# Attention: score maxima of two key chunks joined in one instruction and moved by a DMA into one row, the next sequence's norm and transposes in small pieces

## What is computed

```python
x = x + mix(norm(x))          # a softmax mixing over tokens, from means of x
x = x + experts(norm(x))      # 8 experts, each picks 256 tokens a sequence
x = x + attention(norm(x))    # 16 heads of 64, causal, then @ w_o
x = x + experts(norm(x))
# attention, per head: a = q k^T / 8, masked above the diagonal
#                      y = softmax(a) v ; out = concat(y) @ w_o
```

## Time and profile before

| | |
|---|---|
| median of 3 runs | 2518.96 us (2515.04 to 2521.3) |
| the profiled execution's own time | 2510.51 us |
| its span in the profile | 2508.7 us |
| mean granted clock of TensorE | 0.947 |
| attention (first transpose of maxima to the last) | 761.0 to 1952.4 us |

### The profile page before, as it was taken

One profiled execution on the slowest core, in us unless ns is written; L12 is line 12 of the kernel. 1 busy time (PEld: TensorE's weight loads), 2 busy tenths in 40 slices (PEclk: granted clock), 3 DMA queues, 4 the chain that ended last, 5 costly groups with the idle time before them and its releaser, 6 DMA issues.

```text
span 2508.7 us, 33816 instructions
## 1 busy us (share of the span) xinstructions
PE 2272.5 (91%) x12104; PEld 1689.4 (67%) x12104; DVE 1564.3 (62%) x3334; ACT 1005.1 (40%) x1900; POOL 1293.3 (52%) x1043
## 2 busy tenths in 40 slices
PE   2888599989979999999999999999999768999997
PEld 1344488879976666676666766567566557888997
DVE  6325368865546777557775577764777444885563
ACT  2311154344434445435454344534455314434443
POOL 1000355566624766546664476644667433656664
PEclk9798689999998999999999999999999798999999
DMA  5131244455532221122111222123221214445552
GB/s 193 38 130 42 85 118 122 115 130 136 122 92 61 53 57 51 51 76 60 51 51 51 76 53 57 51 68 100 72 73 34 76 36 142 120 100 135 145 125 51
DMA packets 148454, 213.25 MB, mean 85 GB/s; under 512 B 19248, under 2 KB 112448, under 8 KB 148288
## 3 DMA queue, kind: packets, MB, share of 16 engines
q1 hardware_dynamic: 123712, 177.51, 23.8%
q0 software_dynamic: 24576, 33.57, 7.8%
HBM read 137.51 MB, written 39.98 MB: 71 GB/s over the span
## 4 chain that ended last, share of the span: by engine, by line
PE 74%; DVE 11%; POOL 5%; issue 5%; DMA 2%; ACT 2%; POOLq 1%; SPq 0%; DVEq 0%; ACTq 0%
PE psum L960 11%; PE psum L939 11%; PE psum L1064 9%; PE psum L988 7%; PE psum L1017 6%; PE psum L1036 5%; PE psum L1047 5%; PE psum L824 4%; PE psum L1085 4%; PE psum L1002 4%; PE psum L1074 2%; POOL t_acc L1762 2%; PE psum L857 1%; DVE f_hhi L1535 1%; PE psum L907 1%
## 5 line engine op out<-in xcount | busy, mean ns | idle before, releaser
L1239 ACT ACTIVATE t_p<-psum 128x512 f32<-128x512 f32 (+3 forms) x768 | 324.8, 491 | 359.9 <-PE psum L1047 354.8
L1762 POOL TENSOR_TENSOR t_acc<-t_acc,t_p 128x1024 f32<-128x1024 f32 (+3 forms) x256 | 415.7, 1624 | 19.2 <-ACT t_p L1239 0.8
L1582 DVE CUSTOM_DVE_ANT_0 psum<-psum,t_mask 128x128 f32<-128x128 f32 (+3 forms) x512 | 240.2, 510 | 150.9 <-PE psum L1017 150.9
L960 PE MATMUL psum<-f_whi,f_hhi 128*128 128x256 f32 x1024 | 299.8, 293 | 20.0 <-DVE f_hlo L1537 19.9
L1535 DVE CAST f_hhi<-f_h 128x512 fp32r<-128x512 f32 x256 | 161.6, 631 | 228.4 <-ACT f_h L1190 227.0
L960 PE MATMUL psum<-f_whi,f_hlo 128*128 128x256 f32 x1024 | 294.0, 287 | 0.0
L960 PE MATMUL psum<-f_wlo,f_hhi 128*128 128x256 f32 x1024 | 293.9, 287 | 0.0
L1064 PE MATMUL psum<-t_p,t_v 128*64 128x512 f32 (+3 forms) x1536 | 291.2, 500 | 1.5 <-POOL t_p L1742 1.5
L1687 POOL TENSOR_TENSOR f_wlo<-f_wst,f_whi 128x1024 fp32r<-128x1024 f32 x64 | 159.4, 2505 | 251.8 <-ACT f_whi L1174 251.7
L1190 ACT ACTIVATE f_h<-psum 128x512 f32<-128x512 f32 x256 | 153.1, 598 | 284.3 <-PE psum L939 249.3
L1762 POOL TENSOR_TENSOR t_acc<-t_p 128x768 f32<-128x768 f32 x64 | 134.9, 2108 | 174.5 <-PE psum L1074 170.1
(11 more groups left out here) (199 smaller groups left out, 4577.2 us busy)
## 6 DMA issues: line engine op xcount, KB each, us to landing
f_wst<-in_L_ffn_w SPq DMA_DIRECT2D x64, 1024.0 KB, 5.5
t_ka<-t_ka SPq DMA_DIRECT2D x64, 256.0 KB, 3.5
t_qb<-t_qa SPq DMA_DIRECT2D x64, 256.0 KB, 3.6
t_wk<-wkT SPq DMA_DIRECT2D x32, 256.0 KB, 4.2
t_wq<-wqT SPq DMA_DIRECT2D x32, 256.0 KB, 4.1
t_wv<-wvT SPq DMA_DIRECT2D x16, 512.0 KB, 4.8
normal<-f_xy SPq DMA_DIRECT2D x5, 1024.0 KB, 6.8
a_x<-in_L_attn_a_x SPq DMA_DIRECT2D x4, 1024.0 KB, 9.7
```

The costliest lines, as they stand in the source:

```text
L960: m = pe.matmul(out, h[:, js], w[:, f, :], start=(f == 0 and a == 0 and j % 2 == 0), stop=(f == FT - 1 and a == 2), skip_group_check=True)
L1239: act.activation(p[:, i, q0:], k.bank[bank][:, q0:], ACT.Exp, scale=1.0 / float(np.sqrt(k.DH))).then_inc(k.drained[bank], 1)
L1582: s = dve.tensor_tensor_reduce(part, part, t["mask"][:, BANK - w:BANK], 1.0, NEG, ALU.add, ALU.max, top)
L1762: pool.tensor_tensor(acc[:, :, q0:], (p0 if kt == 1 else acc)[:, :, q0:], p[:, :, q0:], ALU.add).then_inc(k.p_acc, 1)
```

## The change

The tiles `pick` and the semaphore `d_max` go; `mx` becomes one plain 128 x 128 tile with the 16 maxima in its first columns, `neg` ([16, 128], two of them) is new, the `qb` of two heads lie side by side in one tile, and `QROWS` is 65. `xres` is no tile of its own any more: its two chunks are the two halves of `xy`. The part of the key chunk with the diagonal takes the maximum of the full chunk, `mx1`, as its start value. `norm` has four steps of two bn_stats instead of two of four, everywhere it is used.

```diff
@@ -226,8 +232,9 @@
         t["rden"] = [sb("t_rden", [P, BANK // 32]) for _ in range(2)]
-        t["mask"], t["pick"] = sb("t_mask", [P, BANK], BF16), sb("t_pick", [NBLK, NBLK, P], BF16)
-        t["mx"] = [sb("t_mx", [P, 2, P // 2]) for _ in range(2)]
+        t["mask"] = sb("t_mask", [P, BANK], BF16)
+        t["neg"] = [sb("t_neg", [2 * NBLK, P], F32R) for _ in range(2)]
+        t["mx"] = [sb("t_mx", [P, P]) for _ in range(2)]
@@ -269,14 +276,24 @@
-        for n in range(self.NBLK):
-            for c in range(n // self.KPC + 1):
-                w = min(BANK, (n + 1) * P - c * BANK)
...
+        first = [(n, 0) for n in range(self.KPC + 1)]
+        rest = [(n + c, 1 - c) for n in range(self.KPC, self.NBLK) for c in (1, 0) if n + c < self.NBLK]
+        for n, c in first + rest:
...
@@ -569,13 +586,15 @@
             self.t_load(b)
+            for _ in range(4):
+                yield
...
         def normalize_results():
+            while state["stored"] < NC * (B - 1):
+                yield
             for b in range(B - 1):
-                while state["stored"] < NC * (b + 1):
-                    yield
@@ -613,9 +632,8 @@
                 state["values"] = project_values(b)
-            if hp == NHP - 2 and b + 1 < B:
+            if hp == NHP - 5 and b + 1 < B:
                 normalizing[b + 1] = normalize(b + 1)
-                extra.append(normalizing[b + 1])
@@ -675,11 +695,14 @@
                 if n == per * u:
+                    finish(n)
                     yield
-                    finish(n)
+                self.high_scores(u, c, kt)
+                if n == per * u:
...
                 yield
+                self.high_scores(u, c, kt + 1)
@@ -709,19 +732,21 @@
                 if place < 8:
-                    for _ in range(1 + (hp == 0 and place < 4)):
-                        pump(products)
+                    pump(products)
...
                     next(state["values"])
-                if 7 < place < 20:
-                    owed += 21 / 12
+                if 5 < place < 20:
+                    owed += 21 / 14
...
                         owed -= 1
+                if u + 1 < U and (place == 22 or (u + 2) % NHP == 0 and place > 19):
+                    pump(coming)
                 if place == 22 and u + 1 < U:
-                    pump(coming)
                     self.max_rows(u + 1)
-                if behind and place % 4 == 0:
+                if u // NHP + 1 in normalizing and place in (0, 2, 4, 6):
+                    pump(normalizing[u // NHP + 1])
+                if behind and place in (0, 2, 4, 6, 10, 14, 20, 21, 23):
@@ -1006,8 +1031,9 @@
         k, pe, t = self.k, self.e, self.k.t
+        if c == 0 and n % k.KPC == 0:
+            self.wait_drained(("qk", u, k.NC + n // k.KPC))
         if (n, c) == (0, 0):
-            self.wait_drained(("qk", u, 2 * k.NC - 1))
@@ -1021,27 +1047,37 @@
         bank = self.take(("rows", u), self.work_bank())
-        self.wait_ge(k.t_const_p, 6)
-        self.wait_ge(k.d_max, u + 1)
-        pe.transpose(k.bank[bank][:, 0:P], t["mx"][u % 2][:].rearrange("p i n -> p (i n)"),
-                     k.ident[:]).then_inc(k.filled[bank], 1)
+        self.wait_ge(k.t_const_p, 4)
+        for n, c, _, heads in k.max_parts():
+            if c == n // k.KPC:
+                self.wait_drained(("max", u, n, c, heads[0]))
+        pe.transpose(k.bank[bank][:, 0:P], t["mx"][u % 2][:], k.ident[:]).then_inc(k.filled[bank], 1)
...
+    def high_scores(self, u, c, kt):
+        k, pe, t = self.k, self.e, self.k.t
+        q0, qs, ks = self.score_slices(c, kt)
+        for i in range(2):
+            bank = self.take(("st", u, c, kt, i), self.work_bank())
+            hd = t["heads"][u % 2][i]
+            pe.matmul(k.bank[bank][:, q0:], hd["ka"][:, ks], hd["qa"][:, qs], start=True, stop=False)
...
         k, pe, t = self.k, self.e, self.k.t
-        banks = [self.take(("st", u, c, kt, i), self.work_bank()) for i in range(2)]
...
-        for i in range(2):
-            hd = t["heads"][u % 2][i]
-            pe.matmul(k.bank[banks[i]][:, q0:], hd["ka"][:, ks], hd["qa"][:, qs], start=True, stop=False)
+        q0, qs, ks = self.score_slices(c, kt)
+        banks = [k.where["st", u, c, kt, i][0] for i in range(2)]
...
             v = min(4 + 2 * hp, 16) - 1
-            self.wait_drained(("rows", u))
...
                 self.wait_ge(k.q_dup[u % 2][h][1], DMA * (u // 2 + 1))
+            self.wait_ge(k.q_rows[u % 2], DMA * (u // 2 + 1))
@@ -1568,36 +1604,31 @@
         k, dve, t = self.k, self.e, self.k.t
-        mx, mx1 = t["mx"][u % 2], t["mx1"]
+        mx, mx1 = k.maxima(u), t["mx1"]
...
             self.wait_filled(("rows", u - 2))
-        if (n, c) == (k.KPC, 1) and u:
-            self.wait_ge(k.d_max, u)
...
         for i in heads:
-            top = mx1[:, i, n - k.KPC:n - k.KPC + 1] if c else mx[:, i, n:n + 1]
...
             if c == n // k.KPC:
-                self.wait_ge(k.t_const_p, 6)
-                s = dve.tensor_tensor_reduce(part, part, t["mask"][:, BANK - w:BANK], 1.0, NEG, ALU.add, ALU.max, top)
+                self.wait_ge(k.t_const_p, 4)
+                if c:
+                    self.wait_drained(("max", u, n, 0, i))
+                s = dve.tensor_tensor_reduce(part, part, t["mask"][:, BANK - w:BANK], 1.0,
+                                             mx1[:, i, n - k.KPC:n - k.KPC + 1] if c else NEG, ALU.add, ALU.max,
+                                             mx[:, i, n:n + 1])
             else:
-                s = dve.tensor_reduce(top, part, AX.X, ALU.max)
+                if u:
+                    self.wait_drained(("max", u - 1, n, 1, k.heads_of(n, 1, i)))
+                s = dve.tensor_reduce(mx1[:, i, n - k.KPC:n - k.KPC + 1], part, AX.X, ALU.max)
         s.then_inc(k.drained[bank], 1)
-        if (n, c, i) == (k.NBLK - 1, 1, 1):
-            for m, d, _, h in k.max_parts():
-                if m >= k.KPC:
-                    self.wait_drained(("max", u, m, d, h[0]))
-            dve.tensor_tensor(mx[:, :, k.KPC:k.NBLK], mx[:, :, k.KPC:k.NBLK], mx1[:], ALU.max).then_inc(k.d_max, 1)
...
         bank = self.wait_filled(("rows", u))
-        for i in range(2):
-            self.wait_ge(k.t_const_p, 6)
...
-            s = dve.tensor_tensor(t["heads"][u % 2][i]["qb"][k.DH:k.QROWS, :].rearrange("p (a b) -> p a b", b=P),
-                                  spread(rows, 1, k.NBLK), t["pick"][:], ALU.mult)
-        s.then_inc(k.drained[bank], 1)
+        if u > 1:
+            self.wait_ge(k.q_rows[u % 2], DMA * (u // 2))
+        dve.tensor_scalar(t["neg"][u % 2][:], k.bank[bank][0:2 * k.NBLK, 0:P], -1.0, None, ALU.mult).then_inc(k.drained[bank], 1)
@@ -1907,7 +1935,8 @@
         else:
-            self.wait_filled(("xT", k.B - 1, 1, 1))
+            for c in range(k.NC):
+                self.wait_ge(k.q_xout[c], DMA * (k.B - 1))
@@ -1924,6 +1953,9 @@
         self.wait_filled(("xT", b - 1, 1, 1))
+        if b > 1:
+            for c in range(k.NC):
+                self.wait_ge(k.q_xout[c], DMA * (b - 1))
@@ -1954,11 +1986,22 @@
+    def max_rows(self, u):
+        k, sp, t = self.k, self.e, self.k.t
+        if u > 1:
+            self.wait_filled(("st", u - 2, 1, 2 * k.KPC - 1, 1))
+        self.wait_drained(("rows", u))
+        row = t["qb"][u % 2][k.DH:k.QROWS, :, :].rearrange("p i (n j) -> p (i n) j", j=P)
+        sp.dma_start(row.bitcast(F32), t["neg"][u % 2][:].bitcast(F32)).then_inc(k.q_rows[u % 2], DMA)
...
         k, sp = self.k, self.e
-        if b:
-            self.wait_ge(k.q_xout[c], DMA * b)
-        sp.dma_start(k.t["xres"][c][:], self.chunk(k.res, b, c)).then_inc(k.q_xres[c], DMA)
+        if b + 1 < k.B:
+            self.wait_filled(("xT", b + 1, 1, 1))
+        else:
+            self.wait_ge(k.q_y[b - 1], DMA * 2)
+        sp.dma_start(k.t["xres"][c], self.chunk(k.res, b, c)).then_inc(k.q_xres[c], DMA)
```

More of the change, by code:

```diff
@@ L208, in attention_tiles, with heads @@
         L, D, NBLK, DT, DH, NHP, KPC = self.L, self.D, self.NBLK, self.DT, self.DH, self.NHP, self.KPC
[L209 removed]
+        t["qb"] = []
+        def heads():
+            qb = sb("t_qb", [P, 2, L], F32R)
+            t["qb"].append(qb)
+            return [dict({n: sb("t_" + n, [P, L], F32R) for n in ("qa", "ka", "kb")}, qb=qb[:, i, :]) for i in range(2)]
         values = lambda: sb("t_v", [P, NBLK, 4 * DH])
@@ L218, in attention_tiles @@
         t["v"].append(values())
-        t["xres"] = [sb("t_xres", [P, KPC, D]) for _ in range(2)]
+        t["xres"] = [t["xy"][:, c * KPC:(c + 1) * KPC, :] for c in range(2)]
         t["stats"], t["mv"], t["rstd"] = (sb("t_stats", [P, NBLK, 6]), sb("t_mv", [P, NBLK, 2]),
@@ L338, in norm @@
         self.runs += 1
-        for half in range(2):
-            self.norm_stats(n, half, x, stats, mv, rstd, ready)
+        for part in range(4):
+            self.norm_stats(n, part, x, stats, mv, rstd, ready)
             yield
@@ L1275, in norm_stats @@
```

(6 more changed lines are left out.)

35 lines of the change are left out of this document (18 added, 17 removed).

## The result

After: 2474.59 us, median of 4 runs (2469.95 to 2480.52). Before beside it: 2517.0 us (2510.6 to 2521.3). The ratio is 0.9835, interval 0.9804 to 0.9866: 1.65% faster, 42 us. In a later comparison of 6 runs against 11 it was 0.9851 (0.9819 to 0.9883). The prediction was 2494 us with a range of 2478 to 2510. The sign was right; the gain was bigger than the range allowed, by 3.4 us. Executions of one kernel scatter by 10 us and more here, and the two profiled ones are 35.0 us apart.

The account below looks back on a forecast made before the run. TensorE, busy 91% of the span, was taken as the bound, others costing only where it waits. Terms 20 + 4.5 + 3 + 2 - 4.5 + 0 = 25 us off 2510.5 gave 2485.5; plus 8.5 to the median, 2494 us, range 2478 to 2510.

Parts of the forecast that it names:

- D: Lighter VectorE in ordinary units: weight loads wait less for the low halves; gain 2 us over 25 units.
- A: Next sequence's norm, in smaller steps and started earlier, stops stalling TensorE in three units; gain 20 us, bounds 11 and 22.
- B: Next sequence's transposes, moved earlier behind other matmuls, no longer make TensorE wait; gain 4.5 us, bounds 0 and 6.5.
- C: Attention's output product, two places later, avoids waits for t_yT and the one put down to issue; gain 3 us.
- E: Last sequence's norms of results: 1 MB loads and a store delay the key doubling; loss 4.5 us, bounds +8 and -10.
- F: New row DMA in every unit, ready at T+2.0 to T+2.9 (T: maxima transpose's start), before the low score matmul; cost 0.
- My own test of that premise: Sign for the whole kernel: VectorE's busy time down 100 us with unchanged span would disprove that TensorE's waits were VectorE's doing.
- the unit interval that I named as proof: Sign for F: ordinary units staying at 34.0 to 34.1 us, the low score matmul at T+2.96 without a DMA wait.
- the row DMA was not late: Rival on the low score matmul's path: landing at 3.5 us gives 2530 us; chance 0.07 slower, 0.04 near break-even.
- the norm didn't stall: Rival on the next sequence's norm: it still stalls in the low halves' window, half of A lost, 2505 us; chance 0.13.
- E didn't gain: Rival on the last sequence's norms: the doubling doesn't stand behind the loads, gain 6 us, total 2483; chance 0.13.
- the loads of t_xy and xres behind it held up none of TensorE's lines: Rival that gains only move: t_xy load delays the doubling, xres makes waits, E goes badly; 2514 us, chance 0.05.

Follow-up runs that it names:

- join alone: The kernel before with only the joined maxima, their new order, the scaling by -1 and the row DMA, old schedule kept: 2513.32 us.
- ballast run: The changed kernel with two idle VectorE products per unit behind the scaling of the maxima: 2519.07 us, before beside it 2524.82.
- the pieces alone: The kernel before with only the new schedule of norm and transposes: 2477.64 us once, later 2486.59 us (6 runs), ratio 0.9883.

## Why the prediction was too careful

The median came out 19.4 us below the forecast of 2494. Of these, 10.0 are the terms: I forecast 25 us, and the profiled executions are 35.0 apart. The other 9.4 are the step from one profiled execution to a median: I added 8.5 us to the sum because before's profiled execution lay that far below its median, and after's lies 1.0 above its own. That 8.5 was scatter taken for an offset. With the terms right and that offset kept, the forecast would have been 2484, so the measured time would still have lain 9 us below it; the medians of 11 and 6 runs later differ by 36.8.

In attention the gain was 40.6, with a loss of 7.0 behind it. The terms, with the ordinary unit's 0.54 us taken out of each row of the table and counted under D:

| part | forecast | measured |
|---|---|---|
| A, norm in small pieces | 20 | 25.9 - 9 x 0.54 = 21.0 |
| B, transposes | 4.5 | 13.3 - 6 x 0.54 = 10.1 |
| C, output two places later | 3 | 2.8 - 4 x 0.54 = 0.6 |
| D, lighter VectorE | 2 | 26 x 0.54 + 3.1 = 17.1 |
| E, norms of results | -4.5 | -4.6 - 7 x 0.54 = -8.4 |
| F, row DMA | 0 | 0 |
| tail | not looked at | -7.0 |

- **The step that failed is D**, sized at 2 us where the profile has 17.1: "the matmul slips about 0.1 us. Over 25 units: gain 2". I took an ordinary unit for TensorE's alone because it was "busy without a break". The ends of matmuls are modelled, so a chain of matmuls that start a little late shows as busy. The one visible sign was the weight load's 0.27 us, which I cut to 0.1; matched matmul by matmul, TensorE lags by 0.28 from there on, and the unit gave 0.54 in all (0.13 of it by the wider spacing of the row maxima, which the forecast didn't price). My own test of that premise was the other way round (VectorE falls, the span doesn't), and the unit interval that I named as proof, 34.0 to 34.1, came out at 33.50. The join alone and the ballast run put the cause in the VectorE work ahead of the low halves, with the ballast's size only roughly matched.
- **A was right in size** by the sum, and in mechanism: in after the waits of L1013 and L1067 for t_kb are 2.2 us where L988 and L1036 had 16.1. Units 5, 13 and 21 take 33.50 us each, where one took 41.47; units 4, 12 and 20 take 0.5 to 0.7 more than ordinary ones, about the 0.5 a sequence that I left for GpSimd's pow. I missed that the new start is also a condition for F: without it the row DMA makes the norm units 12.0 us longer (the join alone), through the load behind it on SyncE. And the pieces alone bring 15, not 20; the rest needs the lighter VectorE that A's text counted as room.
- **B was mis-sized**: 10.1 against 4.5, above its bound of 6.5. The place is worth 4.0 when VectorE is light and 6.6 when it isn't; the rest is D again, in units in which VectorE has more to do.
- **C** brought 0.6, since its last wait was 2.2 us and not nothing, and it made the tail longer.
- **E was right in mechanism, and low.** In unit 25 I had the doubling issued near T+7.5 and landed at T+18.8, and a stall from T+14.6, 4.2 us long; in unit 28 a stall of 5.7 to 7.6. Timelines of SyncE and TensorE in after; T is 1687.31 and 1802.41:

```profile
1694.50 0.38 SPq L1940 DMA_DIRECT2D t_xy<-out  x1
1694.99 1.17 SPq L1987 DMA_DIRECT2D t_ka<-t_ka  x2
1706.26 0.66 PE L1043 MATMUL psum<-t_ka,t_qa 128*128 128x128 f32 x2 [4.27 <-DMA t_ka<-t_ka]
...
1803.97 0.53 SPq L1945 DMA_DIRECT2D normal<-t_xy  x1
1808.43 0.38 SPq L1940 DMA_DIRECT2D t_xy<-out  x1
1808.91 1.18 SPq L1987 DMA_DIRECT2D t_ka<-t_ka  x2
1818.56 0.66 PE L1043 MATMUL psum<-t_ka,t_qa 128*128 128x128 f32 x2 [4.66 <-DMA t_ka<-t_ka]
```

  The first is right to 0.2 us (doubling issued at T+7.68, TensorE on at T+18.95, 4.27). The second is 1.0 short of the low end, since the store landed in 4.5 us and TensorE went on 9.7 us behind the doubling's issue. The loss was 8.4 and not 4.5, near the far bound of 10. Beside the 8.9 us of stalls there is a lower clock: 0.92 in units 25 and 28 and 0.95 in unit 29, where the other four have 1.00. Units 26 and 27 are 1.9 and 1.4 us longer than with the loads held back, at full clock, and that isn't explained. The windows (columns as in the earlier trace rows) of the unit shown above and of 44 us from the first load on:

```profile
1160.28:1193.76 33.48, 33.30 (x178) 22.42 (x177) 24.45 (x63) 16.78 (x36) 22.94 (x22) 1.00 0.20 48
1694.00:1738.00 44.00, 39.13 (x190) 26.82 (x188) 27.34 (x75) 17.80 (x39) 24.67 (x22) 0.92 0.26 61
```

- **F was right.** Scaling 0.28 us against 0.25, issue at T+0.62 against T+0.6, landing 1.8 us, inside the 1.4 to 2.3 of the two small transfers, and far from the doublings' 3.5. In three of the edits (join alone, norm as before, row maxima as before) one or two waits for the row appear, of 0.7 us at most; in after none. An estimate from the fixed 2.0 us of the Trainium skill's page DMA: Bandwidth & Descriptors (the anatomy of a DMA; fitted there for GpSimd's queue) would have put the row at T+2.6 and hidden it too; the measured landing of 1.8 us is 0.2 below it.
- **The tail** stands in no step. I ended every sum at the last transpose of maxima, and two idle steps per output block, with something that stays open, moved work past it.
- The rivals: the row DMA was not late; the norm didn't stall; E didn't gain; the loads of t_xy and xres behind it held up none of TensorE's lines. The range held no case in which D and B gave *more* than the waits in TensorE's list. (That list sums to about 38 us, not to "some 30".)

## What to carry to other kernels

When an engine that is not the bottleneck gets lighter just before it frees the bottleneck's buffers, measure the period of the steady loop and don't rest on the list of waits: slips too short for TensorE's list of waits were the largest mis-sized term here, and the weight loads' waits, or the same matmul's offset from a marker in two kernels, show them. Before a small DMA is put on a queue, list what is issued behind it and how soon that is needed; its own landing was free, the load behind it cost 12 us until it was started earlier. And follow each delayed step to the end of the last iteration, where nothing is left to hide it.

## What the runs showed of the hardware

- Two 256 KB SBUF transfers, issued 0.5 and 1.1 us behind a 1 MB load on the same queue, landed 8.3 to 10.6 us after their issue (three pairs, one in before and two in after), against a median of 3.5. An 8 KB transfer into one partition with no bulk ahead landed in 1.8 us (median of 32; at most 2.3).
- The ballast's two operands both came from SBUF. GpSimd's product for t_yT, 1.28 us in before and after alike, took 2.26 us beside it (median of 23), and each idle product took 1.2 to 2.2 us (median 1.57). L1598, with one operand in PSUM, had left the same GpSimd line at 1.27 in the 27 units in which the two overlapped. The Trainium skill's page SBUF — State Buffer (two separate sides) has VectorE and GpSimd exclude each other for whole instructions when VectorE reads two operands from SBUF and GpSimd reads SBUF too. The trace agrees with that in kind, and it may be why the ballast weighed 3.5 us instead of 2.4; a ballast with a PSUM operand wasn't run.
- The time before the first transpose of maxima varied by 16 us between executions of kernels that are the same there (756.5 to 772.9), while intervals inside attention repeated to 0.3 us.
